# Two edge counts in a byte and four nodes in a PSUM sum, in a four-layer graph network on one core

## The reference

```
deg = segment_sum(ones, dst);  norm = where(deg > 0, deg ** -0.5, 0)
def step(h):                       # 10 times
    h = h * norm
    h = segment_sum(h[src], dst, num_segments=12500)
    h = h * norm
    return 0.9 * h + 0.1 * feat_0
```

## Time and profile before

| | |
|---|---|
| time, median of 3 runs | 23347.96 us (23346.12 to 23353.0) |
| profiled execution | 23347.1 us, span 23345.2 us |
| busy share: TensorE, VectorE, ScalarE, GpSimd | 70%, 49%, 15%, 50% |
| keys of the counts | about 556 to 764 us of the span |
| chunk 0 counted | about 769 to 1000 us |
| loop of layer 0, with the counts of chunks 1 to 24 | about 1161 to 7124 us |
| loop of layer 1 | about 7322 to 13180 us |
| loop of layer 2, with the counts of chunks 25 to 48 | about 13534 to 17490 us |
| first propagation step | 17758 to 18337 us |
| nine further steps | 18358 to 23306 us |

### The profile page before, as it was taken

One profiled execution on the slowest core, in us unless ns is written; L12 is line 12 of the kernel. 1 busy time (PEld: TensorE's weight loads), 2 busy tenths in 40 slices (PEclk: granted clock), 3 DMA queues, 4 the chain that ended last, 5 costly groups with the idle time before them and its releaser, 6 DMA issues. The chain is left out here.

```text
span 23345.2 us, 238245 instructions
## 1 busy us (share of the span) xinstructions
PE 16346.0 (70%) x62077; PEld 9394.6 (40%) x62077; DVE 11520.3 (49%) x20173; ACT 3537.8 (15%) x5816; POOL 11600.8 (50%) x10131
## 2 busy tenths in 40 slices
PE   0266655555554888888888555555555999999999
PEld 0144443334332333333333233333333555655565
DVE  1476554444445999999999633333337400000000
ACT  0022222222220111111111111111110000000000
POOL 2378888888884555555555477777771000000000
PEclk7665555555555555555555577878887999999999
DMA  7133444443443222222222145555555788888888
GB/s 245 36 42 40 43 43 42 42 42 39 42 42 50 43 45 45 44 44 45 45 44 45 27 99 113 111 112 114 112 104 176 270 287 286 287 287 288 283 280 267
DMA packets 4274312, 2714.62 MB, mean 116 GB/s; under 512 B 3013401, under 2 KB 3973279, under 8 KB 4271231
## 3 DMA queue, kind: packets, MB, share of 16 engines
q1 hardware_dynamic: 2316670, 2104.96, 31.1%
q0 software_dynamic: 670848, 221.33, 9.5%
q10 hardware_dynamic: 1286162, 380.64, 7.4%
HBM read 2307.21 MB, written 462.84 MB: 119 GB/s over the span
## 5 line engine op out<-in xcount | busy, mean ns | idle before, releaser
L2642 PE MATMUL pacc<-ring,HB 128*97 128x512 fp8e4 (+1 forms) x24500 | 5250.7, 377 | 316.6 <-PEq L2635 277.1
L2090 PE MATMUL pR<-w,H 65*128 65x384 f32 x6272 | 4523.7, 876 | 1109.5 <-PEq L2088 1107.9
L1840 POOL DMA_INDIRECT xg<-d_tab,s_i x3136 | 3027.6, 965 | 2945.3 <-POOLq L1838 1996.8
L2642 PEld LDWEIGHTS pacc<-ring,HB 128*97 128x97 bf16 x24500 | 3056.3, 126 | 2476.9 <-issue 357.8
L2340 POOL DMA_INDIRECT xag<-d_xa,s_i x3136 | 3002.0, 957 | 967.2 <-issue 837.5
L2090 PEld LDWEIGHTS pR<-w,H 65*128 65x128 f32 x6272 | 1839.2, 324 | 3462.9 <-issue 3457.7
L1370 POOL DMA_INDIRECT d_acc<-T,ix x1568 | 2479.6, 1581 | 499.3 <-issue 462.1
L1370 POOL DMA_INDIRECT d_acc<-AG,ix x1568 | 2468.5, 1574 | 516.9 <-issue 419.8
L2676 DVE TENSOR_TENSOR hq<-pt,norm 128x384 f32<-128x384 f32 (+1 forms) x90 | 46.8, 520 | 4612.9 <-DVEq L2673 4612.9
L1653 PE MATMUL pm<-ms,eq 128*128 128x32 f32 x6272 | 1367.2, 400 | 1060.0 <-PEq L1651 1059.6
L1653 PEld LDWEIGHTS pm<-ms,eq 128*128 128x128 f32 x6272 | 1346.2, 330 | 1105.9 <-issue 1105.7
(11 more groups left out here) (298 smaller groups left out, 17210.2 us busy)
## 6 DMA issues: line engine op xcount, KB each, us to landing
ring<-d_A SPq DMA_DIRECT2D x1120, 1344.0 KB, 6.5
d_A<-stage ACTq DMA_DIRECT2D x96, 1568.0 KB
row<-d_m SPq DMA_DIRECT2D x1568, 64.0 KB
wrow<-d_w SPq DMA_DIRECT2D x196, 512.0 KB, 5.5
d_scan<-so ACTq DMA_DIRECT2D x392, 256.0 KB
d_exp<-zt ACTq DMA_DIRECT2D x32, 1568.0 KB, 19.6
xe<-d_exp SPq DMA_DIRECT2D x196, 256.0 KB
xg<-d_tab,s_i POOLq DMA_INDIRECT x3136
```

Of the source, the lines that this page charges most:

```text
L1840: e.indirect_dma_start(out=xg[k][:, t, :], out_offset=None, in_=d_tab, in_offset=bass.IndirectOffsetOnAxis(ap=s_i[n][:, t:t + 1], axis=0)) ...
L2090: last = e.matmul(pR[u % 2][:, j, 0:384], H[k][:, (2 * u + j) * P:(2 * u + j + 1) * P], w2[:, :], start=True, stop=True)
L2642: end = e.matmul(pacc[q % 2][j // 512][:, 0:n], HB[i][:, c * CB + bb, :], ring[r][:, j // AC:(j + n) // AC, bb, :], start=(c == 0 and bb = ...
```

## The change

A window now has WN = 16 nodes, and four nodes share a PSUM sum: an edge counts 1, 16, 256 or 4096 by its node, so that the uint16 on ScalarE holds four counts of four bits. A byte of `d_A` holds nodes 2i (low half) and 2i+1 (high half), and the matrix has half its bytes (BY = 128 for a chunk's row and source block). Windows of 16 nodes need fewer slots: by `slots_of` chunk 0 has 497 (before 525), the loop of layer 0 has 2608 (3136), the loop of layer 2 has 1440 (1632); NS is 4608 and NSB 36. A window in the loops is made in two halves, so that the loops still have 32 units for each chunk. The operands `ok` keep their 392 columns.

In every propagation step, the first too, VectorE takes the nibbles of a piece apart into `nodes`, with one AND for the low halves and one shift with AND for the high halves. TensorE reads `nodes`, whose 512 columns are now four runs of 128 bytes (before two of 256). ScalarE puts the nodes back in order as it writes `OT`, with steps of two words. `packed` has 3 buffers of two pieces (a load has the bytes that it had), `nodes` has 3 buffers of a piece. The pass over `bits` and its test are gone: the degree test stays.

```diff
-WN = 8
+WN = 16
 AC = 256
+BY = AC // 2
-KW = WN // 2 * NB
+KW = WN // 4 * NB
...
-                    e.tensor_scalar(other[:, :], k0, float(P), None, ALU.is_ge).then_inc(S("vc"), 1)
+                    e.tensor_scalar(other[:, :], k0, float(2 * P), None, ALU.is_ge).then_inc(S("vc"), 1)
...
-                    e.scalar_tensor_tensor(k0, other[:, :], -float(P), k0, ALU.mult, ALU.add).then_inc(S("vc"), 1)
+                    e.scalar_tensor_tensor(k0, other[:, :], -float(2 * P), k0, ALU.mult, ALU.add).then_inc(S("vc"), 1)
                     e.tensor_scalar(k1, other[:, :], 255.0, 1.0, ALU.mult, ALU.add).then_inc(S("vc"), 1)
...
+                    e.tensor_scalar(other[:, :], k0, float(P), None, ALU.is_ge).then_inc(S("vc"), 1)
...
+                    e.scalar_tensor_tensor(k0, other[:, :], -float(P), k0, ALU.mult, ALU.add).then_inc(S("vc"), 1)
+                    e.tensor_scalar(other[:, :], other[:, :], 15.0, 1.0, ALU.mult, ALU.add).then_inc(S("vc"), 1)
...
+                    e.tensor_tensor(k1, k1, other[:, :], ALU.mult).then_inc(S("vc"), 1)
...
-            def step_sp(e, ring, free):
+            def step_sp(e):
                 at = 0
                 for q in range(NPASS):
                     n = width(q) * P // AC
-                    for c in range(NCH):
...
+                    for c in range(NCH // 2):
+                        r = at % RB
+                        e.wait_ge(S(f"fab{r}"), 1)
+                        e.sem_inc(S(f"fab{r}"), -1)
+                        e.dma_start(packed[r][:, 0:n, :, :].rearrange("p n b m -> p n (b m)"),
+                                    d_A[q * PW // AC:q * PW // AC + n, :, c * 2 * CB * BY:(c + 1) * 2 * CB * BY]
...
+            def unpack(e, q, at):
+                r, u, half, n = at // 2 % RB, at % RN, at % 2, width(q) * P // AC
+                if half == 0:
+                    e.wait_ge(S(f"ab{r}"), 16)
+                    e.sem_inc(S(f"ab{r}"), -16)
+                e.wait_ge(S(f"fun{u}"), 1)
+                e.sem_inc(S(f"fun{u}"), -1)
+                both = packed[r][:, 0:n, half * CB:(half + 1) * CB, :].bitcast(I32)
+                low, high = (nodes[u][:, s, 0:n, :, :].bitcast(I32) for s in range(2))
+                e.tensor_scalar(low, both, SMALL, None, ALU.bitwise_and)
+                e.tensor_scalar(high, both, 4, SMALL, ALU.logical_shift_right, ALU.bitwise_and).then_inc(S(f"un{u}"), 1)
...
+                        u = at % RN
+                        e.wait_ge(S(f"un{u}"), 1)
+                        e.sem_inc(S(f"un{u}"), -1)
+                        if at % 2 == 1:
+                            e.sem_inc(S(f"fab{at // 2 % RB}"), 1)
...
-                                               ring[r][:, j // AC:(j + n) // AC, bb, :], start=(c == 0 and bb == 0),
+                                               counts[u][:, :, j // AC:(j + n) // AC, bb, :], start=(c == 0 and bb == 0),
...
-                        end = e.activation(OT[q % 2][:, j:j + n], pacc[q % 2][j // 512][:, 0:n], ACT.Copy)
+                        end = e.activation(OT[q % 2][0:97, j:j + n].rearrange("p (k i s) -> p s k i", s=2, i=BY),
+                                           pacc[q % 2][j // 512][0:97, 0:n].rearrange("p (s k i) -> p s k i", s=2, i=BY),
+                                           ACT.Copy)
...
                 for q in range(NPASS):
-                    if look is None:
-                        finish(q)
-                        continue
                     for c in range(NCH):
-                        look(q, q * NCH + c)
+                        unpack(e, q, q * NCH + c)
                         if q and c == 3:
                             finish(q - 1)
-                if look is not None:
-                    finish(NPASS - 1)
+                finish(NPASS - 1)
...
-            RB = 6
+            RB = RN = 3
```

More of the change, by code:

```diff
@@ L42 @@
 SMALL = 0x0F0F0F0F
-LARGE = -0x0F0F0F10
 BYTE = 512.0
@@ L971, in count_load, with half_window, count_ones @@
             e.dma_start(A["kt"][h][:, :, 0:m], d_key[:, :, bass.ds(at + m * h, m)]).then_inc(S(f"n_kt{h}"), 16)
-        def count_ones(e, A, n, w):
-            h, r, s = w // (WPC // 2), w % RU, w % (WPC // 2) * n
+        def half_window(n, u):
+            first = -(-n // 2)
+            return first if u % 2 == 0 else n - first
+        def count_ones(e, A, n, u):
+            w, r, m = u // 2, u % RU, half_window(n, u)
+            h, s = w // (WPC // 2), w % (WPC // 2) * n + u % 2 * half_window(n, 0)
             if s == 0:
@@ L985, in count_ones, with count_sums, count_out @@
             last.then_inc(S("n_oh"), 1)
-        def count_sums(e, A, n, w):
-            e.wait_ge(S("n_fpw"), 1)
-            e.sem_inc(S("n_fpw"), -1)
+        def count_sums(e, A, n, u):
+            w, m = u // 2, half_window(n, u)
+            if u % 2 == 0:
+                e.wait_ge(S("n_fpw"), 1)
+                e.sem_inc(S("n_fpw"), -1)
             e.wait_ge(S("n_oh"), 1)
             e.sem_inc(S("n_oh"), -1)
-            for i in range(n):
-                last = e.matmul(A["pw"][w % 2][:, 0:KW], A["ol"][w % RU][:, i, :], A["ok"][w % RU][:, i, :],
-                                start=(i == 0), stop=(i == n - 1))
+            for i in range(m):
+                last = e.matmul(A["pw"][w % 2][:, 0:KW], A["ol"][u % RU][:, i, :], A["ok"][u % RU][:, i, :],
+                                start=(u % 2 == 0 and i == 0), stop=(u % 2 == 1 and i == m - 1))
             last.then_inc(S("n_pw"), 1)
-        def count_out(e, A, c, w):
+        def count_out(e, A, c, u):
+            w = u // 2
             h, v = w // (WPC // 2), w % (WPC // 2)
-            if v == 0:
+            if v == 0 and u % 2 == 0:
                 e.wait_ge(S(f"n_sg{h}"), 16)
@@ L2617, in back @@
                     for j in range(width(q)):
-                        end = e.matmul(pt[q % 2][:, j, :], OT[q % 2][:, j * P:(j + 1) * P], three[:, :],
+                        end = e.matmul(pt[q % 2][:, j, :], OT[q % 2][0:97, j * P:(j + 1) * P], three[:, :],
                                        start=True, stop=True)
@@ L2666, in step_act, with step_dve @@
                     e.sem_inc(S(f"facc{q % 2}"), 1)
-            def step_dve(e, i, last, look=None, check=None):
+            def step_dve(e, i, last, check=None):
                 def finish(q):
@@ L2717, in own @@
                             e.sem_inc(S(f"{name}{r}"), -1)
-            RB = 6
+            RB = RN = 3
             LOOP = (KS - 2) // 2
-            assert (KS - 2) % 2 == 0 and NPASS * NCH % RB == 0
+            assert (KS - 2) % 2 == 0 and NPASS * NCH % (2 * RB) == 0 and NPASS * NCH % RN == 0
             with ExitStack() as part:
-                ring8 = [sb(part, f"ring{r}", [P, PW // AC, CB, AC], U8) for r in range(RB)]
-                ring = [r[:, :, :, :].bitcast(FP8) for r in ring8]
-                bits = sb(part, "bits", [P, PW // AC, CB, AC], U8)
-                bad = sb(part, "bad", [P, NB + 1])
+                packed = [sb(part, f"packed{r}", [P, PW // AC, 2 * CB, BY], U8) for r in range(RB)]
+                nodes = [sb(part, f"nodes{u}", [P, 2, PW // AC, CB, BY], U8) for u in range(RN)]
+                counts = [u[:, :, :, :, :].bitcast(FP8) for u in nodes]
+                bad = sb(part, "bad", [P, NB])
                 mr = sb(part, "mr", [P, 1])
                 go = sb(part, "go", [P, 1], I32)
-                def free(e, r):
-                    e.wait_ge(S(f"fab{r}"), 1)
-                    e.sem_inc(S(f"fab{r}"), -1)
                 with nc.Block() as block:
@@ L2849, in _ @@
                         own(e, ("fab",), RB, 1)
-                        steps(e, lambda i, last: step_sp(e, ring8, free))
+                        steps(e, lambda i, last: step_sp(e))
                         own(e, ("fab",), RB, -1)
@@ L2855, in _ @@
                         own(e, ("facc", "fpt"), 2, 1)
-                        steps(e, lambda i, last: step_pe(e, ring, i), lambda: e.sem_inc(S("hb"), NPASS))
+                        steps(e, lambda i, last: step_pe(e, i), lambda: e.sem_inc(S("hb"), NPASS))
                         own(e, ("facc", "fpt"), 2, -1)
@@ L2861, in _ @@
                         own(e, ("fot",), 2, 1)
-                        steps(e, lambda i, last: step_act(e, ring))
+                        own(e, ("fun",), RN, 1)
+                        steps(e, lambda i, last: step_act(e))
                         own(e, ("fot",), 2, -1)
+                        own(e, ("fun",), RN, -1)
                     @block.vector
```

102 lines of the change are left out of this document (39 added, 63 removed).

## The result

The changed kernel takes 23396.7 us (median of 15 runs, 23390.1 to 23402.1) beside 23346.6 us for the kernel before (15 runs, 23340.7 to 23353.0): a ratio of 1.0021, 95% interval 1.0013 to 1.0029. The forecast was 23337 us, and its range reached to 23405. The kernel is 50 us slower where 11 us less were expected, and the sign is beyond doubt.

A forecast was written before the change was run, and what follows sets the result against it. TensorE was taken to bound the steps (531 of 532 us), GpSimd's issues the loops of layers 0 and 2. Terms -28 - 11 - 39.8 + 34 + 23 + 1.7 + 9 = -11 us gave 23337 us, range 23280 to 23405.

The forecast's parts named there:

- the two new instructions: VectorE's AND and shift with AND in each step: 0.86 us each, 1.7 us a full piece with semaphores.
- The rival of a slower matmul: TensorE's matmuls slow on four runs of 128 bytes; at 5% of the pace 23600 us; chance 0.10.
- Before the loops: Index lists, key gathers, VectorE's key work, key storing and chunk 0 with fewer slots: -28 us in sum.
- Wait before step 1: Piece 0 must be loaded (9.23 us) and then taken apart before step 1: +1.7 us.
- First step: First propagation step becomes like the others, with cheaper inspection and test but `bits` cleared: -39.8 us.
- Last pass: TensorE waits for VectorE's `finish` in the last pass: eight steps at 4.2 us, the last at 0.5, +34 us.
- boundaries: Between steps, `finish` precedes taking piece 0 apart: +3.1 us four times, +2.7 four times at returns; +23 us.
- ScalarE's copy: Copy writing every second word, seen ahead of `back` and at the end: 0 to 18 us, middle +9 taken.
- The two loops: Loops of layers 0 and 2 lose 528 and 192 slots: -7 and -4 us, bounds 0 and -24.
- The case of slower: Whole kernel slower by over 0.2%, through slower matmuls, VectorE late in every pass, or a tail: chance 0.21.
- The new waits don't come: Halved bytes free boundaries that waited for loads, or edge loops gain from fewer slots: 23280 us; chance 0.15.
- a late VectorE: VectorE late in every pass if a pair takes over 3.6 us; at 4.6 us 23410 us; chance 0.06.

The follow-up runs named there:

- the run with the new order: Changed kernel with 80 more VectorE instructions, finishing the last-but-one pass after the last pass's pieces, three next-step pieces taken apart earlier: 23222.5 us, ratio 0.9948.
- the first four experiments: Changed kernel with 80 or 128 more VectorE instructions, kernel before with 80 more, changed kernel with old tensor places: ratios to kernel before 0.9978, 0.9979, 1.0002, 0.9979.

## Why the prediction was wrong

- **What bounds a step, the matmul's pace, the two new instructions.** Right: 0.86 us an instruction, a DMA share of 0.43, TensorE at 531 of 532 us. The rival of a slower matmul didn't come.
- **Before the loops**, -28: -32.4. **Wait before step 1**, +1.7: +1.7. **First step**, 551.0 us: 551.8 from the first matmul to the last `back` (17774.19 to 18325.95). With the part ahead of it and the test, -39.8: -38.8.
- **Last pass, +34, and boundaries, +23.** Right in mechanism: the run with the new order took both away. The last passes measure +34.3, but the agreement is in part luck: the waits are 27.6 and not 34, and the lower clock that the sum hasn't got adds 5.8. The boundaries measure +26.5. Their returns have 9.8 to 10.0 for 8.3, and the 6 us that the kernel before had there were read as a wait for the load, which they weren't: TensorE's own stream stands still behind its branch, before the change as after it.
- **ScalarE's copy, +9.** Mis-sized: 0.1 us a step at most, so the lower end of its bounds. It makes up for the boundaries, so that the steps come to 62.5 for 66.
- **The two loops, -7 and -4.** The first is mis-sized: 32 us, beyond the bound of 24; the second has 8.7. The argument read GpSimd's pace off windows of different density, where comparisons differ, and those are worth 8; it left out the stores of counts, which the run with twice the stores shows to lengthen the loop.
- **The sum.** The failed step is the one that isn't in it. "In the two loops" are those of layers 0 and 2, in which counts are made; layer 1's loop was taken at nothing because no line of it changes. It went from 118.48 to 120.49 us a turn, +93 us from first to last gather, because 838 more instructions ahead of it moved it across four packets of VectorE's instruction stream. Without that step the change is 46.7 - 93.3 = -46.6 us; the changed kernel with 80 instructions more measures 52.8 less than before.
- **The rivals and the range.** The case of slower had two mechanisms, both in the steps, and neither happened. "The new waits don't come" was wrong, though its other half (the loops gain from fewer slots) came in part. That 23396.7 lies inside the range of 23280 to 23405 is luck: that end was drawn for a slower matmul and a late VectorE.

The Trainium skill has a rule for it, in "Runtime: NRT & Kernel Launch" (Instruction fetch mechanics): each engine has a small buffer for instructions, by that page 32 KiB for most and 128 KiB for TensorE, filled in order by a DMA queue of its own, and a branch to something outside of what it holds has to fetch it first. The trace agrees on the mechanism: VectorE's body in layer 1 is 330 x 64 B = 21 KB, stays resident across three packets and doesn't across four. It doesn't agree on the sizes: VectorE's packets are 8192 B here, 16384 B are queue 8's, and four packets of 8192 B would be the page's 32 KiB and yet aren't held. The rule would have made layer 1's loop a rival; the price, 1.5 to 2.5 us a turn, had to come from a run.

## What to carry to other kernels

Count the instructions of each engine in every loop. If three packets of 128 stay and four don't, as in the one loop tested here, a body of about 256 to 384 instructions fits or not by where it starts: adding or removing code anywhere ahead of it can cost 2 us a turn in a loop that nobody touched, and as many idle instructions as bring it back cost nothing. The row to look at is the instruction queue's in the stretch of the loop: one packet in 5500 us against 227. A loop whose gathers, or anything else, already set the pace can hide the loss, as the first four experiments did, so read the packets and not the time alone. The long work of an engine that takes over a job between two others (here taking bytes apart) loses its cover where passes are narrow; put the next pieces ahead of the long work there before judging the change: in that order, and with the loop in its place, this change is 121 us faster than before, and not 50 slower.

## What the runs showed of the hardware

- A loop of 330 instructions on VectorE, 118.4 to 118.5 us a turn, took 1.5 us (half the gathers), 2.0 us (the changed kernel) and 2.5 us (the kernel before with 80 more) longer when its instructions were fetched again, five packets of 8192 B a turn, though the fetches are 0.1% of the DMA engines' time.
- The place in the stream decides it: +80 instructions took the packets away from one kernel and brought them to the other; +128 changed nothing.
- When gathers set the pace (129 us a turn), the same fetches cost at most some 16 us in 47 turns (6308.4 us without, 6298.6 to 6326.5 with), and the kernels with and without them differ by 4 us or less in all.
- TensorE's first entry behind the return of its loop in the propagation steps came 5.8 to 6.4 us late at nine of nine returns in three kernels, each time 2.4 us behind the start of a packet of 16384 B; inside the body the same entry isn't late.
- In the narrow last passes, after `back` with its short matmuls and waits, the granted clock was 0.50 to 0.53 for about 3 us, and again behind a wait of 3.3 us: 14 matmuls of 256 columns took 3.20 us.
- ScalarE writing every second fp32 word, 97 x 512 a copy: 634 for 597 ns. TensorE, which waits for it after three copies, waits 0.07 us longer.
- Making every store of counts twice (packets of 64 B; 27.3 MB more from 2800 to 6900 us) slows 1568 pairs of scatters on GpSimd by 49 to 56 us in 5860 (one execution), while the median scatter stays at 1556 ns; the maximum grows from 2308 to 2512.
